# Local attention in a four-layer sequence kernel: probabilities turned by products with diagonal matrices

## What is computed

```
def attn_layer(x, Wqkv, qs, ksc, Wo):            # 16 heads of 64
    q, k, v = jnp.split(x @ Wqkv, 3, -1)          # after a split into heads:
    q = l2norm(q) * qs
    k = l2norm(k) * ksc
    q = q * cos * scale + rotate_half(q) * sin * scale
    k = k * cos * inv + rotate_half(k) * sin * inv
    out = local_attention(q, k, v)                # windows of 32
    return out @ Wo

def local_attention(q, k, v):                     # each query sees its window and the one before
    sim = jnp.einsum('bhwie,bhwje->bhwij', bq, bk2) * QK_SCALE
    sim = jnp.where(mask, -jnp.finfo(sim.dtype).max, sim)
    attn = jax.nn.softmax(sim, -1)
    return jnp.einsum('bhwij,bhwje->bhwie', attn, bv2)
```

## Time and profile before

| | before |
|---|---|
| median of three runs | 5864.99 us |
| profiled execution | 5863.58 us |
| its span, first to last instruction | 5861.5 us |
| TensorE busy | 5288.7 us (90%) |
| GpSimd busy | 3853.1 us (66%) |
| ScalarE busy | 3898.0 us (67%) |
| VectorE busy | 3779.4 us (64%) |
| first windowed transformer, about | 680 to 2760 us of the span |
| second windowed transformer, about | 2900 to 4985 us of the span |

### The profile page before, as it was taken

One profiled execution on the slowest core, in us unless ns is written; L12 is line 12 of the kernel. 1 busy time (PEld: TensorE's weight loads), 2 busy tenths in 40 slices (PEclk: granted clock), 3 DMA queues, 4 the chain that ended last, 5 costly groups with the idle time before them and its releaser, 6 DMA issues. The chain is left out here.

```text
span 5861.5 us, 119540 instructions
## 1 busy us (share of the span) xinstructions
PE 5288.7 (90%) x41154; PEld 3784.2 (65%) x41154; DVE 3779.4 (64%) x13691; ACT 3898.0 (67%) x11502; POOL 3853.1 (66%) x3058
## 2 busy tenths in 40 slices
PE   7886699999999999998699999999999999697989
PEld 5674366666666666666366666666666666464678
DVE  4454577777777777776667777777777776454522
ACT  2211388888888888887478888888888888122333
POOL 0000588888888888886488888888888887230000
PEclk9996799999999999999899999999999999797999
DMA  0000000000000000000000000000000000000000
GB/s 12 23 1 3 22 1 12 10 10 9 4 12 10 12 10 1 16 5 1 26 1 12 10 1 16 6 12 10 12 10 1 16 5 1 5 2 4 2 30 8
DMA packets 30947, 53.31 MB, mean 9 GB/s; under 512 B 7688, under 2 KB 17168, under 8 KB 29712
## 3 DMA queue, kind: packets, MB, share of 16 engines
q1 hardware_dynamic: 30352, 45.66, 2.5%
HBM read 44.60 MB, written 1.05 MB: 8 GB/s over the span
## 5 line engine op out<-in xcount | busy, mean ns | idle before, releaser
L1744 PE MATMUL bank<-wA,next_rowT 128*128 128x512 f32 x2304 | 1169.9, 623 | 138.6 <-DVE turnB L2099 66.7
L1953 ACT ACTIVATE pairs<-pairs,negmax 128x128 f32<-128x128 f32 (+1 forms) x3072 | 1244.4, 427 | 12.1 <-DVE negmax L2060 11.1
L1932 POOL TENSOR_TENSOR big<-big,neg_half 128x16 f32<-128x16 f32 x384 | 1117.5, 2910 | 0.0
L1920 POOL TENSOR_TENSOR turnA<-raw,ropes 128x512 f32<-128x512 f32 x768 | 971.1, 1275 | 169.6 <-ACT raw L1977 141.5
L2060 DVE CUSTOM_DVE_ANT_0 pairs<-bank,bands,big 128x128 f32<-128x128 f32 (+1 forms) x3072 | 941.3, 363 | 87.6 <-PE bank L1676 78.3
L1927 POOL TENSOR_TENSOR qk<-turnA,turnB 128x512 f32<-128x512 f32 x768 | 978.4, 1274 | 0.0
L288 POOL TENSOR_TENSOR rstd<-vareps,neg_half 128x2 f32<-128x2 f32 x56 | 39.0, 696 | 1144.5 <-DVE vareps L259 721.6
L1744 PEld LDWEIGHTS bank<-wA,next_rowT 128*128 128x128 f32 x2304 | 377.0, 190 | 562.5 <-issue 241.1
L1960 ACT ACTIVATE pairsT<-bank 128x512 f32<-128x512 f32 x768 | 472.7, 616 | 303.4 <-PE bank L1689 303.2
L1953 ACT ACTIVATION_READ_ACCUMULATOR pairs<-pairs,negmax 128x1 f32 x3072 | 654.5, 213 | 0.0
L1904 POOL COPY spread<-recip 128x256 f32<-128x256 f32 x768 | 306.8, 400 | 348.3 <-DVE recip L2069 342.2
(11 more groups left out here) (306 smaller groups left out, 11414.7 us busy)
## 6 DMA issues: line engine op xcount, KB each, us to landing
wA<-in_wt_wqkv SPq DMA_DIRECT2D x72, 256.0 KB, 2.8
wB<-in_wt_wo SPq DMA_DIRECT2D x12, 512.0 KB, 3.3
wC<-in_wt_w SPq DMA_DIRECT2D x12, 341.0 KB, 2.9
wD<-in_wt_w SPq DMA_DIRECT2D x12, 192.0 KB, 2.4
big<-in_e_up SPq DMA_DIRECT2D x1, 2048.0 KB
big<-in_e_down SPq DMA_DIRECT2D x1, 2048.0 KB
scl<-in_wt_scales SPq DMA_DIRECT2D x12, 128.0 KB, 3.2
X<-in_x SPq DMA_DIRECT2D x8, 128.0 KB, 2.4
```

The costliest lines, as they stand in the source:

```text
L1744: pe.matmul(side_bank(i)[:, :], c.next_rowT[:, t * P:(t + 1) * P], wqkv[:, k * 512:(k + 1) * 512], start=True, stop=True).then_inc(s.chunk ...
L1920: g.tensor_tensor(c.turnA[:, m % 2, :].rearrange("p (h d) -> p h d", h=8), c.raw[:, m % 4, :].rearrange("p (h d) -> p h d", h=8), cos, ALU ...
L1932: g.tensor_tensor(norms_of(rs[q % 2], m)[:, :, which, :], norms_of(ss, m)[:, :, which, :], c.neg_half[:, 0:16].rearrange("p (t h) -> p t h ...
L1953: last = a.activation(tile, tile, ACT.Exp, scale=-1.0, bias=c.negmax[:, 2 * p + side, t:t + 1], accum_out=c.pair_sums[:, p % 4, t, side:si ...
```

## The change

The reciprocals no longer go through GpSimd, TensorE and ScalarE to the contexts. Instead VectorE multiplies four copies of the identity by the reciprocals of the four tiles of a pair (`dve_diagonals`): four diagonal matrices. TensorE multiplies the probabilities by them, which turns and scales them in one (`pe_turn_probs`), VectorE scales the small corner of the previous window with a product of its own, and the contexts are only copied out (`dve_copy_ctx`). Turning, copying and weighing come one slot later than before, and the scores now stand first in TensorE's slot. GpSimd's spreading, TensorE's turning of the shares and ScalarE's copy of them go away.

```diff
-        def pe_turn_probs(pe, T, p):
-            pe.wait_ge(s.probs_ready, T * PAIRS + p + 1)
-            if T * PAIRS + p > T0 * PAIRS:
-                pe.wait_ge(s.probsT_ready, T * PAIRS + p)
+        def pe_turn_probs(pe, n):
+            p = n % PAIRS
+            pe.wait_ge(s.diagonals_ready, n + 1)
+            if n > first_pair:
+                pe.wait_ge(s.probsT_ready, n)
             for side in range(2):
                 probs, out = c.pairs[:, 2 * (p % 4) + side, :], c.bank[2][:, S * side:S * side + S]
-                pe.transpose(out[:, 0:P], probs[:, 0:P], c.ident[:, :])
-                last = pe.transpose(out[:, P:2 * P], probs[:, P + WINDOW:2 * P + WINDOW], c.ident[:, :])
+                pe.matmul(out[:, 0:P], probs[:, 0:P], c.diagonals[:, p % 2, side, :], start=True, stop=True,
+                          skip_group_check=True)
+                last = pe.matmul(out[:, P:2 * P], probs[:, P + WINDOW:2 * P + WINDOW], c.diagonals[:, p % 2, 2 + side, :],
+                                 start=True, stop=True, skip_group_check=True)
             last.then_inc(s.probsT_in_psum, 1)
...
         def pe_window(pe, T):
             following = has_turn(T + 1)
             for p in range(PAIRS):
-                pe_turn_probs(pe, T, p)
-                if p >= 1:
-                    pe_shares(pe, T, p - 1)
-                elif has_turn(T - 1):
-                    pe_shares(pe, T - 1, PAIRS - 1)
+                n = T * PAIRS + p
                 if p + 2 < PAIRS:
                     pe_scores(pe, T, p + 2)
                 elif following:
                     pe_scores(pe, T + 1, p + 2 - PAIRS)
+                if has_pair(n - 1):
+                    pe_turn_probs(pe, n - 1)
                 if p == 0 and following:
                     pe_xT(pe, T + 1)
-                if p >= 1:
-                    pe_weigh(pe, T, p - 1)
-                elif has_turn(T - 1):
-                    pe_weigh(pe, T - 1, PAIRS - 1)
+                if has_pair(n - 2):
+                    pe_weigh(pe, n - 2)
...
-                act_copy_probs(a, T, p)
+                if has_pair(T * PAIRS + p - 1):
+                    act_copy_probs(a, T * PAIRS + p - 1)
...
-                if p >= 1:
-                    act_copy_shares(a, T, p - 1)
-                elif has_turn(T - 1):
-                    act_copy_shares(a, T - 1, PAIRS - 1)
...
+        def dve_diagonals(v, n):
+            p = n % PAIRS
+            v.wait_ge(s.probs_ready, n + 1)
+            recip = c.recip[:, 0, 4 * (p % 4):4 * (p % 4) + 4]
+            v.reciprocal(recip, c.pair_sums[:, p % 4, :, :].rearrange("p t h -> p (t h)")).then_inc(s.recip_ready, 1)
+            if has_pair(n - 2):
+                v.wait_ge(s.probsT_in_psum, n - 1)
+            v.wait_ge(s.recip_ready, n + 1)
+            v.tensor_tensor(c.diagonals[:, p % 2, :, :], c.ident[:, :].unsqueeze(1).broadcast_to((P, 4, P)),
+                            recip.unsqueeze(2).broadcast_to((P, 4, P)), ALU.mult).then_inc(s.diagonals_ready, 1)
+            prev = c.pairs[0:WINDOW, 2 * (p % 4):2 * (p % 4) + 2, P:P + WINDOW]
+            v.tensor_tensor(prev, prev, recip[0:WINDOW, 2:4].unsqueeze(2).broadcast_to((WINDOW, 2, WINDOW)),
+                            ALU.mult).then_inc(s.prev_scaled, 1)
+
+        def dve_copy_ctx(v, n):
+            T, p = n // PAIRS, n % PAIRS
+            v.wait_ge(s.ctx_in_psum, n + 1)
+            v.tensor_copy(ctxT[T % 2][:, p, :], c.bank[4 + p % 2][:, 0:S]).then_inc(s.ctx_ready, 1)
...
-                dve_recip(v, T, p)
-                if p >= 2:
-                    dve_share(v, T, p - 2)
-                elif has_turn(T - 1):
-                    dve_share(v, T - 1, p + PAIRS - 2)
-                dve_turn_prev(v, T, p)
+                if has_pair(T * PAIRS + p - 3):
+                    dve_copy_ctx(v, T * PAIRS + p - 3)
+                if has_pair(T * PAIRS + p - 1):
+                    dve_turn_prev(v, T * PAIRS + p - 1)
...
                     dve_negmax(v, T + 1, p + 2 - PAIRS)
+                dve_diagonals(v, T * PAIRS + p)
...
                     for p in range(PAIRS):
-                        pool_spread(g, T, p)
```

More of the change, by code:

```diff
@@ L132, in allocate @@
     c.pair_sums = sb("pair_sums", [P, 4, HALVES, 2])
-    c.shares = sb("shares", [P, 2, S])
     c.recip = sb("recip", [P, 2, 32])
-    c.spread = sb("spread", [P, 2, S])
+    c.diagonals = sb("diagonals", [P, 2, 4, P])
     c.ctx = sb("ctx", [P, HALVES, D])
@@ L2054, in dve_negmax @@
             v.sem_inc(s.scores_seen, 1)
+            if has_pair(T * PAIRS + p - 4):
+                v.wait_ge(s.probsT_in_psum, T * PAIRS + p - 3)
             if p % 4 == 0:
@@ L2209, in dve_tail @@
             L = T1 - 1
-            dve_share(v, L, PAIRS - 2)
-            dve_share(v, L, PAIRS - 1)
+            dve_turn_prev(v, end_pair - 1)
+            for n in range(end_pair - 3, end_pair):
+                dve_copy_ctx(v, n)
             dve_ff_add(v, L - 2)
```

60 lines of the change are left out of this document (23 added, 37 removed).

## The result

The kernel after takes 6878.78 us (median of four, 6877.35 to 6879.56), the kernel before 5864.78 us (median of four): 1.173 times as long [1.171, 1.175]. The direction was forecast; the 6535 us were 344 short, and the measured time lies above the range, which ended at 6830. The profiled execution's span is 6877.6 us.

A forecast was written before the change was run, and what follows sets the result against it. The prediction took a loop of TensorE and VectorE (8.83 us from slot 3's keys' copy to slot 5's chunk) as the bound; 0.9 + 1.76 + 0.72 + 0.66 + 1.42 plus blocking 1.6, 7.06 x 95 = 671 us, gave 6535 us, range 6250 to 6830.

The forecast's parts named there:

- order and missing shares: Waits moved in slots 6, 7 and 0, less TensorE's 0.31 us saving in six slots: 0.94 us a turn, 89 us.
- TensorE's real products: Four real float32 matmuls a slot (0.89 us) for four transposes (0.43), in six slots: 262 us.
- What bounds the kernel: A loop each turn: TensorE from slot 5 to slot 3 of the next turn, then 8.83 us of VectorE.
- TensorE, "+0.15 us a slot": Net of real matmuls, old transposes and dropped shares in six slots where TensorE leads: +0.9 us a turn.
- the shares' 0.31: TensorE's two transposes of the shares in each slot, 0.31 us, counted as saved.
- VectorE, "+1.76 on the loop": Two product groups, slots 3 and 4, between keys' copy and slot 5's chunk, 0.88 us a slot: +1.76 us a turn.
- Blocking +1.6: VectorE's new products wait for GpSimd's wide operations in slots 4 and 5: +1.6 us a turn (0 to 4.8).
- the power function's exception: GpSimd's power function doesn't block VectorE's product in slot 3; without the exception another 1.5 us a turn.
- Rival 2: GpSimd wins every time: blocking 4.8 us a turn instead of 1.6, 6838 us; chance 0.21.
- The moved waits: New TensorE waits: +0.72 us before slot 6's scores, +0.66 before the gates, +1.42 before slot 0's scores.

The follow-up runs named there:

- order: Kernel after without VectorE's products and with transposes against the identity for the real products, the division by the sums left out: 6107.7 us, 1.041 times the kernel before.
- real products: Kernel after without VectorE's two products, constant identity tiles in place of the diagonals, TensorE's real matrix products kept: 6366.6 us, 1.085 times the kernel before.
- VectorE's products with nothing beside them: Kernel after with GpSimd's cosine product, sum and keys' scaling cut to 64 of 512 columns: 6482.1 us, 1.105 times the kernel before.
- the run with the filler: Kernel after with 18 extra useless identity transposes in TensorE's slot 6, ahead of the scores that wait there: 6770.5 us, 1.154 times the kernel before.
- the products in the kernel before: Kernel before with VectorE also making a 128x512 and a 32x64 product each slot into tiles that nothing reads: 6243.5 us, 1.064 times the kernel before.
- the two reorderings: Kernel after with TensorE's turning ahead of the scores and VectorE's rotations of slots 4 and 5 moved ahead, normalisation behind them: 6602.6 us, 1.126 times before.
- the swap alone: Kernel after with TensorE turning the previous pair's probabilities ahead of the scores in every slot: 6470.6 us, 1.103 times the kernel before.

## Why the prediction was right in direction and 344 us short

The forecast had the mechanism: TensorE's busy share in a turn fell to 86% (forecast some 85), line 2063 is blocked (0.88 us in the mean), and the waits in slots 6 and 0 are there. What failed is the size of three terms: what TensorE saves without the shares (order step, 154 us more than forecast), the blocking (137 more) and the clock, which stood at nothing (108). VectorE's products, 52 us less than forecast, made up for a part.

The runs make a chain from one kernel to the other: before 5865, order 6108, real products 6367, VectorE's products with nothing beside them 6482, blocking 6771 (the run with the filler), clock 6879. The second step and the last change one thing each; the first is the order and the missing shares together. The third and the fourth meet in the run in which GpSimd's wide operations are cut as well, so the 115 us are rather too small and the 289 too large, by an amount that no run measured.

| step | predicted us | measured us |
|---|---|---|
| order and missing shares | 0.94 x 95 = 89 | 243 |
| TensorE's real products | 2.76 x 95 = 262 | 259 |
| VectorE's products, unblocked | 1.76 x 95 = 167 | 115 |
| held back by GpSimd | 1.6 x 95 = 152 | 289 |
| clock | 0 | 108 |
| sum | 671 | 1014 |

- *What bounds the kernel* was right: VectorE's operations in slots 3 to 5 lengthen the turn (the products in the kernel before, +379, some 106 of it slower matmuls), and moving some of them behind the rotations gives 68 us back.
- *TensorE, "+0.15 us a slot"* failed: it is +0.43. I took both prices from rows in the middle of a long run of like matmuls, or with one hand-over in them. After, a slot has three hand-overs (0.09 before the scores, 0.11 at the first product, 0.09 at the last) where it had one of 0.09; I took the old one off with the shares' 0.31 and added none. Six slots x 0.28 x 95 are 160 us, the largest miss. It shows in the table's first step, where the saving of the shares stands; the difference between a product and a transpose was right.
- *VectorE, "+1.76 on the loop"* was somewhat high; unblocked it cost 115 us, 1.2 a turn, as far as the run with short GpSimd operations shows it.
- *"Blocking +1.6"* had the mechanism, and the power function's exception held. The odds failed: I let half an operation pass in slots 4 and 5 and the small product lose once in four. The rows show three losses of about 1.08 in the typical turn, 3.25 x 95 = 309 us against 289 by the runs. Rival 2 took five losses and priced 4.8 a turn. Its 6838 us lie nearer the measured time than the forecast, but by luck: its blocking is some 1.6 us a turn too high, and the time came from hand-overs and clock, which it didn't have.
- *The moved waits* (gates, slot 0, scores of slot 6 apart from blocking) were right within 0.15 us each.
- *The clock* was no step at all. The prediction forecast a wait of 0.72 in slot 6; with the blocking behind it the wait became 2.33, and that brought the half clock in two turns of three.

The steps are read in one order; taken in the other, the real products cost 291 us with the products there, against 259 without. The 32 us between them belong to no single step, and as the clock was low on both sides of the 291, they aren't a clean measure of the pair either.

## What to carry to other kernels

Price an operation in the neighbourhood in which it will stand: the first and last of a group that follows another kind of work cost half as much again to nearly twice the steady pitch here (0.33 against 0.22 us, 0.21 against 0.11). Where two engines hold each other back, don't multiply odds: lay the two orders side by side and count whole operations lost, since a loop that repeats meets the same neighbour every turn. And when a change opens a new wait on TensorE, price the clock behind it, and look for work that can be moved into the wait before anything else.

## What the hardware showed that I had not expected

- TensorE got faster by being given 1.96 us of useless transposes a turn: 6770.5 against 6878.8 us. The granted clock was 0.50 behind 57 of 87 waits of 2.33 us and 1.00 behind 28 of them. It was low in nearly every turn behind the 1.89 us of the two reorderings (0.65 in the mean over the 4.8 us that followed in the turn shown), and 1.00 behind the 1.46 us of the swap alone.
- A VectorE product of one tile by a column was held back by GpSimd, as one of two tiles was (0.28 us in the median, up to 1.82).
- A 32x32 product costs VectorE 0.22 us unblocked, a 32x64 one of two tiles 0.20: two such pieces cost 0.44 in place of 0.20.
